# The last tile's embedding rows gathered in two halves of 64 rows per field

## The chip, the core and the metric

The kernel runs on one core of one Trainium2 chip. The metric is the device time of one execution in microseconds (us); lower is better. The core has TensorE (PE, matrix products; its weight loads are shown as PEld), VectorE (DVE), ScalarE (ACT), GpSimd (POOL) and SyncE (SP), and 16 DMA engines that all queues share. Each engine works through its own list of instructions in order, and semaphores order the engines against each other.

## The reference

A recommendation model's top. For each of 512 samples, 26 embedding rows of 128 floats are looked up, one dense row is added, and the products of all pairs of these 27 vectors (351 numbers) and the dense row go through three layers.

```python
e = jnp.stack([tbl_0[ids[:, 0]], ..., tbl_25[ids[:, 25]]], axis=1)     # 512 x 26 x 128
combined = jnp.concatenate([e, r_dense_x[:, None, :]], axis=1)
interact = jnp.einsum('bfd,bgd->bfg', combined, combined)
z = interact[:, _TRIU_I, _TRIU_J]                                      # 512 x 351
h = jnp.concatenate([z, r_dense_x], axis=1)
h = jnp.maximum(h @ W_top1 + b_top1, 0.0)
h = jnp.maximum(h @ W_top2 + b_top2, 0.0)
y = h @ W_top3
```

## The kernel before

The batch is cut into 4 tiles of 128 samples (TILES, P). Ten fields with small tables (LOOK_FIELDS) are looked up on TensorE for all tiles at once: whole tables are brought in, DVE and ACT make one-hot matrices, and PE multiplies (look_up, line 286). That fills the first half of the run. The other 16 fields (GATHER_FIELDS, NG = 16) are gathered by GpSimd: for each tile and field one indirect DMA (line 262) fetches 128 rows of 512 bytes, row p of the tile to partition p of `rows`, by the row numbers in one column of `ids_rows`. These 64 gathers start when `ids_rows` has landed (one transfer at the head of SP's queue, line 225) and follow each other with no other wait, tile 0 first. They are all that GpSimd does after its constants.

Sixteen fields are four groups of four (GROUP = 4, NGROUPS = 4). `rows_landed[t][g]` counts 16 for each gather of a group. `turn(t, g)` on PE waits for 16 * GROUP of it (line 305), turns the four 128x128 blocks (line 307) into PSUM, and ACT's `save_turn(t, g)` copies them into `vecs` (line 597). When all four groups of a tile are saved, `gram` makes the pair products (line 321), DVE's `pack` transposes and picks them (lines 489 and 503), `turn_pairs` (line 344) turns them, and the three layers follow: `layer1_dense` (332), `layer1_pairs` (352), `layer2` (362), `layer3` (371).

The order on PE is written out by hand and interleaves tiles. For the last tile (t = 3) it is: gram(2, 1), layer3(1), turn(3, 0), keep_clock(2), turn_pairs and layer1_pairs of tile 2, turn(3, 1), layer2(2, both), turn(3, 2), layer1_dense(3), layer3(2), turn(3, 3), gram(3, both), keep_clock(4), and then the pairs and layers of tile 3 alone to the end. `keep_clock` (line 377) multiplies zeros so that PE isn't idle while DVE packs. ACT's order is by hand too: save_turn(3, 0) stands ahead of save_pairs(2), save_turn(3, 1) ahead of save_h2(2), save_turn(3, 3) ahead of save_pairs(3). SP's last instruction waits for all four tiles' results (y_saved) and writes them out (line 247).

Of the kernel before, what the change touches and what calls it, by code (L numbers as in the profile page):

```python
# [7 lines left out]
I32 = mybir.dt.int32  # L8
# [3 lines left out]
P = 128  # L12
TILES = 4
# [9 lines left out]
GATHER_FIELDS = [f for f in range(FIELDS) if f not in LOOK_FIELDS]  # L23
NL = len(LOOK_FIELDS)
NG = len(GATHER_FIELDS)
# [32 lines left out]
GROUP = 4  # L58
# [51 lines left out]
def turn_index(t, g):  # L110

    return 1 + t * NGROUPS + g


def build(nc, ids_gather, ids_look, x, tables, looks, w1, b1, w2, b2, w3, out):
    with ExitStack() as ctx:
        def sb(name, shape, dt=F32):
            return ctx.enter_context(nc.sbuf_tensor(name, shape, dt))

        def sem(name):  # L120
            return ctx.enter_context(nc.semaphore(name))
# [2 lines left out]
        zeros = sb("zeros", [P, P])  # L124
        row_ids = sb("row_ids", [P, len(CHUNK_KINDS), MAX_CHUNKS])
        minus_ids = sb("minus_ids", [P, len(CHUNK_KINDS), MAX_CHUNKS])
        ids_rows = sb("ids_rows", [P, TILES * NG], I32)
        ids_wide = sb("ids_wide", [P, WIDE_HELD, 2 * BATCH], I32)

        with nc.sbuf_tensor("table", [P, ARENA, D], F32) as table:  # L130
# [5 lines left out]
        rows = sb("rows", [P, TILES * NG, D])  # L136
# [26 lines left out]
        rows_landed = [[sem(f"rows_landed{t}_{g}") for g in range(NGROUPS)] for t in range(TILES)]  # L163
# [86 lines left out]
        @block.gpsimd  # L250
        def _(pool):
            for n, chunks in enumerate(CHUNK_KINDS):
                nc.gpsimd.iota(row_ids[:, n, 0:chunks], pattern=[[1, chunks]], base=0, channel_multiplier=chunks,
                               allow_small_or_imprecise_dtypes=True).then_inc(consts_ready, 1)
            nc.gpsimd.memset(ident[:], 0.0).then_inc(blank, 1)
            pool.wait_ge(blank, 1)
            nc.gpsimd.affine_select(out=ident[:], in_=ident[:], compare_op=ALU.not_equal, fill=1.0, base=0,
                                    pattern=[[-1, P]], channel_multiplier=1).then_inc(consts_ready, 1)
            pool.wait_ge(ids_landed, 16)
            for t in range(TILES):  # L260
                for i in range(NG):
                    nc.gpsimd.indirect_dma_start(  # L262
                        rows[:, t * NG + i, :], None, tables[GATHER_FIELDS[i]],
                        bass.IndirectOffsetOnAxis(ap=ids_rows[:, t * NG + i:t * NG + i + 1], axis=0)
                    ).then_inc(rows_landed[t][i // GROUP], 16)

        @block.tensor
        def _(pe):
            def look_up(j):

                if j >= 2:
                    pe.wait_ge(look_saved, j - 1)
                head = HEAD_STEPS if j == 0 else 1
                order = [(f, name, k) for name in ("high", "low") for f in range(2) for k in range(head)]
                order += [(f, name, k) for k in range(head, STEPS[j]) for f in range(2) for name in ("high", "low")]
                for f, name, k in order:
                    i = 2 * j + f
                    if f == 0 and name == "high":
                        if k < DVE_STEPS[j]:
                            pe.wait_ge(hot_dve, DVE_STEP0[j] + k + 1)  # L280
                        else:
                            pe.wait_ge(hot_act, ACT_STEP0[j] + k - DVE_STEPS[j] + 1)
                    if k == 0:
                        pe.wait_ge(high_ready if name == "high" else low_ready, i + 1)
                    weights = part(high if name == "high" else low, i)[:, k, :]
                    mm = nc.tensor.matmul(look_ps[:, j % 2 * 2 + f, :], weights,  # L286
                                          onehot[:, (STEP0[j] + k) % RING, f * BATCH:(f + 1) * BATCH],
                                          start=(name == "high" and k == 0),
                                          stop=(name == "low" and k == STEPS[j] - 1))
                    if f == 1 and name == "low":  # L290
                        mm.then_inc(step_used, 1)
                    if j == COUPLES - 1 and f == 1 and name == "low" and k % 2 == 1 and k < 2 * NGROUPS:
                        turn(0, k // 2)
# [7 lines left out]
            def turn(t, g):  # L301
                n = turn_index(t, g)

                pe.wait_ge(turn_saved, n - 1)
                pe.wait_ge(rows_landed[t][g], 16 * GROUP)
                for i in range(GROUP):
                    mm = nc.tensor.transpose(turn_ps[:, n % 2, i * P:(i + 1) * P],  # L307
                                             rows[:, t * NG + g * GROUP + i, :], ident[:])
                mm.then_inc(turned, 1)
# [82 lines left out]
            for j in range(1, COUPLES):  # L392
                look_up(j)

            turn(1, 0)
            pe.wait_ge(look_saved, COUPLES)
            pe.wait_ge(last_look_saved, 1)
            gram(0, 0)
            turn(1, 1)
            pe.wait_ge(w1_landed, 16)  # L400
            layer1_dense(0)
# [326 lines left out]
```

## Time and profile before

| | us |
|---|---|
| median of 3 runs | 114.54 (114.31 to 116.4) |
| the profiled execution | 115.43 |
| its span, first to last instruction | 113.6 |
| PE busy | 100.8 (89% of the span) |
| PEld busy | 84.9 (75%) |
| POOL busy | 68.6 (60%) |
| DVE busy, ACT busy | 53.2, 49.1 |

The profiled execution spent 115.43 - 113.6 = 1.83 us outside the span. Times in the views count from the first instruction. Idle time of an engine that doesn't set the end costs nothing, so the views to read are those that say what the engine on the path waited for, and when each transfer was in place.

### The profile page before, as it was taken

What the parts mean: (1) busy time and instruction counts of PE and PEld (TensorE: products, weight loads), DVE (VectorE), ACT (ScalarE), POOL (GpSimd) and SP (SyncE); (2) the same over time, 40 slices, a digit from 0 to 9 for tenths busy, and PEclk for the clock granted to TensorE, in tenths of its full rate; (3) what the DMA queues carried; (4) which work ended last, traced back from release to release, by engine and by line L of the source; (5) the groups of instructions that cost most, each with busy time, mean ns of one, the idle gap of its engine ahead of it and who ended that gap; (6) DMA issues with size and microseconds to landing.
All of it is one profiled execution on the core that took longest, in us unless ns stands there. A gap on an engine that the chain in (4) does not pass through costs nothing.

```text
span 113.6 us, 3435 instructions
## 1 busy us (share of the span) xinstructions
PE 100.8 (89%) x1538; PEld 84.9 (75%) x1538; DVE 53.2 (47%) x108; ACT 49.1 (43%) x73; POOL 68.6 (60%) x72
## 2 busy tenths in 40 slices
PE   6957999999975999999998969999999989883992
PEld 6943788888854788688778759887989789682890
DVE  1019989999949685980010083116220443007130
ACT  4422553994374759529942151015331313500122
POOL 3277777777778777877777777777677730000000
PEclk9999589999997699999999999999999999999999
DMA  2999955947962899411211221221222210000000
GB/s 77 349 358 398 369 192 163 265 141 239 319 239 48 244 389 344 135 46 46 72 49 52 59 68 46 52 72 49 52 46 74 53 46 0 6 6 0 6 0 1
DMA packets 6001, 14.68 MB, mean 129 GB/s; under 512 B 1889, under 2 KB 2913, under 8 KB 5858
## 3 DMA queue, kind: packets, MB, share of 16 engines
q1 hardware_dynamic: 3650, 9.22, 22.4%
q0 software_dynamic: 2048, 4.20, 14.4%
q10 hardware_dynamic: 288, 1.05, 2.6%
q8 instruction: 12, 0.20, 0.7%
q14 instruction: 3, 0.02, 0.1%
HBM read 14.45 MB, written 0.00 MB: 127 GB/s over the span
## 4 chain that ended last, share of the span: by engine, by line
PE 68%; DMA 10%; ACT 8%; issue 6%; DVE 5%; SPq 0%; DVEq 0%
PE look_ps L286 27%; PE gram_ps L321 12%; PE look_ps L352 10%; PE look_ps L362 7%; DMA ids_wide<-ids_look_dram 6%; PE turn_ps L307 5%; DMA table<-tbl_dram 4%; PE look_ps L332 3%; ACT apart L573 3%; ACT onehot L576 3%; DVE onehot L481 2%; DVE dots L489 2%; PE look_ps L344 1%; PE look_ps L371 1%; PE look_ps L377 1%
## 5 line engine op out<-in xcount | busy, mean ns | idle before, releaser
L262 POOL DMA_INDIRECT rows<-tbl_dram,ids_rows x64 | 67.7, 1058 | 22.6 <-issue 19.2
L286 PE MATMUL look_ps<-onehot,high 128*128 128x512 f32 x88 | 35.6, 421 | 4.4 <-ACT onehot L576 2.4
L286 PE MATMUL look_ps<-onehot,low 128*128 128x512 f32 x88 | 34.5, 415 | 0.0
L481 DVE TENSOR_SCALAR onehot<-ids_wide,row_ids 128x1024 fp32r<-128x1024 int32 x37 | 25.8, 748 | 9.0 <-DMA ids_wide<-ids_look_dram 6.7
L286 PEld LDWEIGHTS look_ps<-onehot,high 128*128 128x128 f32 x88 | 17.1, 197 | 9.7 <-ACT onehot L576 3.2
L286 PEld LDWEIGHTS look_ps<-onehot,low 128*128 128x128 f32 x88 | 18.1, 205 | 3.9
L559 ACT CAST high<-table 128x1024 fp32r<-128x1024 f32 (+1 forms) x10 | 11.2, 1136 | 8.8 <-DMA table<-tbl_dram 8.8
L489 DVE STREAM_TRANSPOSE dots<-gram_ps 128x352 f32<-128x352 f32 (+2 forms) x12 | 5.6, 465 | 19.7 <-PE gram_ps L321 19.7
L471 DVE TENSOR_TENSOR low<-table,high 128x1024 fp32r<-128x1024 f32 (+1 forms) x10 | 13.1, 1319 | 2.5 <-ACT high L559 2.5
L321 PE MATMUL gram_ps<-vecs 128*27 128x27 f32 x1024 | 12.8, 195 | 1.6 <-ACT vecs L597 0.7
L321 PEld LDWEIGHTS gram_ps<-vecs 128*27 128x27 f32 x1024 | 10.9, 108 | 3.8 <-issue 1.1
L597 ACT COPY vecs<-turn_ps 128x512 f32<-128x512 f32 x16 | 9.3, 592 | 9.0 <-PE turn_ps L307 8.9
L352 PE MATMUL look_ps<-pairs_t,w_sb 128*128 128x128 f32 x96 | 12.0, 276 | 0.2 <-ACT pairs_t L603 0.2
L352 PEld LDWEIGHTS look_ps<-pairs_t,w_sb 128*128 128x128 f32 x96 | 11.5, 193 | 0.5 <-ACT pairs_t L603 0.5
L573 ACT ACTIVATE apart<-ids_wide,minus_ids 128x1024 f32<-128x1024 int32 x7 | 8.1, 1152 | 5.3 <-PE look_ps L286 4.0
L307 PE MATMUL turn_ps<-ident,rows 128*128 128x128 f32 x64 | 9.8, 278 | 0.0
L307 PEld LDWEIGHTS turn_ps<-ident,rows 128*128 128x128 f32 x64 | 7.2, 141 | 1.5 <-issue 0.4
L362 PE MATMUL look_ps<-h,w_sb 128*128 128x128 f32 x64 | 8.3, 280 | 0.0
L362 PEld LDWEIGHTS look_ps<-h,w_sb 128*128 128x128 f32 x64 | 7.6, 191 | 0.3 <-DVE h L516 0.2
L576 ACT ACTIVATE onehot<-apart 128x1024 fp32r<-128x1024 f32 x7 | 7.4, 1061 | 0.2
L583 ACT COPY vecs<-look_ps 128x1024 f32<-128x1024 f32 x4 | 4.4, 1091 | 6.8 <-PE look_ps L286 6.8
L608 ACT ACTIVATE h<-look_ps,b_sb 128x128 f32<-128x128 f32 x8 | 2.5, 364 | 9.2 <-PE look_ps L352 9.2
(37 smaller groups left out, 53.5 us busy)
## 6 DMA issues: line engine op xcount, KB each, us to landing
ids_wide<-ids_look_dram SPq DMA_DIRECT2D x5, 512.0 KB, 4.0
table<-tbl_dram SPq DMA_DIRECT2D x4, 640.0 KB, 5.5
table<-tbl_dram SPq DMA_DIRECT2D x4, 512.0 KB, 10.4
table<-tbl_dram ACTq DMA_DIRECT2D x2, 512.0 KB, 5.3
rows<-tbl_dram,ids_rows POOLq DMA_INDIRECT x64, 3.5
w_sb<-w_dram SPq DMA_DIRECT2D x1, 1024.0 KB, 8.5
w_sb<-w_dram SPq DMA_DIRECT2D x1, 512.0 KB, 7.6
x_rows<-x_dram SPq DMA_DIRECT2D x1, 256.0 KB, 10.0
```

Source lines behind the costliest of these rows:

```text
L262: nc.gpsimd.indirect_dma_start(rows[:, t * NG + i, :], None, tables[GATHER_FIELDS[i]], bass.IndirectOffsetOnAxis(ap=ids_rows[:, t * NG + i ...
L286: mm = nc.tensor.matmul(look_ps[:, j % 2 * 2 + f, :], weights, onehot[:, (STEP0[j] + k) % RING, f * BATCH:(f + 1) * BATCH], start=(name == ...
L307: mm = nc.tensor.transpose(turn_ps[:, n % 2, i * P:(i + 1) * P], rows[:, t * NG + g * GROUP + i, :], ident[:])
L321: mm = nc.tensor.matmul(gram_ps[32 * j:32 * j + SLOTS, b, q * SLOTS:(q + 1) * SLOTS], v, v, start=True, stop=True)
L352: mm = nc.tensor.matmul(h1_cols(n), w1_sb[:, c, n * P:(n + 1) * P], pairs_t[:, c, :], start=False, stop=(c == PAIR_CHUNKS - 1), skip_group ...
L362: mm = nc.tensor.matmul(look_ps[:, m, 0:P], w2_sb[:, n, m * P:(m + 1) * P], h1[:, n, :], start=(n == 0), stop=(n == N1 - 1))
L471: nc.vector.tensor_tensor(part(low, i), part(table, i), part(high, i).bitcast(F32), ALU.subtract).then_inc(low_ready, 1)
L481: nc.vector.tensor_scalar(onehot[:, q % RING, :], ids_wide[:, j % WIDE_HELD, :], row_ids[:, kind(j), k:k + 1], None, ALU.is_equal).then_in ...
L559: copy(part(high, i), part(table, i)).then_inc(high_ready, 1)
L573: nc.scalar.activation(apart[:], ids_wide[:, j % WIDE_HELD, :], ACT.Abs, bias=minus_ids[:, kind(j), k:k + 1]).then_inc(apart_ready, 1)
L576: nc.scalar.activation(onehot[:, q % RING, :], apart[:], ACT.Relu, bias=1.0, scale=-1.0).then_inc(hot_act, 1)
L597: copy(tile_vecs(t, slice(s, s + GROUP)), turn_ps[:, n % 2, :].rearrange("p (s b o) -> p b s o", s=GROUP, o=2)).then_inc(turn_saved, 1)
```

## The change

For tile 3 each field is gathered by two indirect DMAs of 64 rows instead of one of 128: first the rows of partitions 0 to 63 for all 16 fields, then those of partitions 64 to 127 for all 16. The row numbers are read from partitions 0 to 63 in both cases, so `ids_rows` has 16 more columns (80 instead of 64), in which the second half's numbers stand at partitions 0 to 63; the host lays them out. `turn(3, g)` waits for twice the count. Tiles 0 to 2 are gathered as before, and the orders on PE, DVE, ACT and SP are the same.

```diff
-        ids_rows = sb("ids_rows", [P, TILES * NG], I32)
+        ids_rows = sb("ids_rows", [P, (TILES + 1) * NG], I32)
...
-            for t in range(TILES):
+            for t in range(TILES - 1):
                 for i in range(NG):
                     nc.gpsimd.indirect_dma_start(
                         rows[:, t * NG + i, :], None, tables[GATHER_FIELDS[i]],
                         bass.IndirectOffsetOnAxis(ap=ids_rows[:, t * NG + i:t * NG + i + 1], axis=0)
+                    ).then_inc(rows_landed[t][i // GROUP], 16)
+
+            t = TILES - 1
+            for half in range(2):
+                for i in range(NG):
+                    at = (t + half) * NG + i
+                    nc.gpsimd.indirect_dma_start(
+                        rows[half * P // 2:(half + 1) * P // 2, t * NG + i, :], None, tables[GATHER_FIELDS[i]],
+                        bass.IndirectOffsetOnAxis(ap=ids_rows[0:P // 2, at:at + 1], axis=0)
                     ).then_inc(rows_landed[t][i // GROUP], 16)
...
-                pe.wait_ge(rows_landed[t][g], 16 * GROUP)
+                pe.wait_ge(rows_landed[t][g], 16 * GROUP * (2 if t == TILES - 1 else 1))
...
+    gather_ids = ids[:, GATHER_FIELDS].reshape(TILES, P, NG)
+    gather_ids = np.concatenate([gather_ids, np.roll(gather_ids[-1:], P // 2, axis=1)])
...
-        "ids_gather": ids[:, GATHER_FIELDS].reshape(TILES, P, NG).transpose(1, 0, 2).reshape(P, -1),
+        "ids_gather": gather_ids.transpose(1, 0, 2).reshape(P, -1),
```

## Rows read from the trace of the kernel before

**Rows 1.** The page: the chain that ended last, by engine.

```profile
PE 68%; DMA 10%; ACT 8%; issue 6%; DVE 5%; SPq 0%; DVEq 0%
```

**Rows 2.** Waits, 86 to 100 us: who waited for whom, us, times, longest.

```profile
ACT vecs L597 <- PE turn_ps L307: 0.7, 2, 0.3
...
PEld turn_ps L307 <- issue: 0.4, 2, 0.2
```

**Rows 3.** The page: the gathers' group (busy, mean ns, idle before) and their queue.

```profile
q0 software_dynamic: 2048, 4.20, 14.4%
...
L262 POOL DMA_INDIRECT rows<-tbl_dram,ids_rows x64 | 67.7, 1058 | 22.6 <-issue 19.2
```

**Rows 4.** Line 262 from 72 to 94 us: ns min/median/max; landing from issue.

```profile
L262 POOL DMA_INDIRECT rows<-tbl_dram,ids_rows x17: 940/944/947, 71.1 to 91.1; - x17
...
DMA to landing us min/median/max: 2.5/2.6/3.5
```

**Rows 5.** Timeline of POOL: first and last of the last tile's 16 gathers.

```profile
72.32 0.94 POOL L262 DMA_INDIRECT rows<-tbl_dram,ids_rows  x1 [0.30 <-issue]
...
91.06 0.94 POOL L262 DMA_INDIRECT rows<-tbl_dram,ids_rows  x1 [0.30 <-issue]
```

**Rows 6.** Timeline, 82 to 114 us, PE's and ACT's instructions around the turns of tile 3.

```profile
88.95 0.60 PE L371 MATMUL look_ps<-h,w_sb 128*1 128x128 f32 x4
...
89.47 0.66 PE L307 MATMUL turn_ps<-ident,rows 128*128 128x128 f32 x4
...
90.78 0.27 ACT L603 COPY pairs_t<-look_ps 128x128 f32<-128x128 f32 x1
...
91.41 1.06 PE L352 MATMUL look_ps<-pairs_t,w_sb 128*128 128x128 f32 x8
...
94.20 0.60 PE L307 MATMUL turn_ps<-ident,rows 128*128 128x128 f32 x4
...
96.42 0.60 PE L307 MATMUL turn_ps<-ident,rows 128*128 128x128 f32 x4
...
98.38 0.66 PE L307 MATMUL turn_ps<-ident,rows 128*128 128x128 f32 x4
...
99.07 0.59 ACT L597 COPY vecs<-turn_ps 128x512 f32<-128x512 f32 x1 [0.33 <-PE turn_ps L307]
99.71 2.35 PE L321 MATMUL gram_ps<-vecs 128*27 128x27 f32 x256 [0.68 <-ACT vecs L597]
```

**Rows 7.** DMA queues from 72 to 94 us: all packets, and the gathers' own.

```profile
DMA packets 550, 1.18 MB, mean 54 GB/s; under 512 B 274, under 2 KB 274, under 8 KB 546
...
q0 software_dynamic: 546, 1.12, 20.4%
```

**Rows 8.** Timeline: GpSimd's shortest instruction, and SP's transfer of the row numbers.

```profile
0.27 0.10 POOL L717 MEMSET const-float32-1.0<- 128x1 f32 x1
...
0.74 0.40 SPq L225 DMA_DIRECT2D ids_rows<-ids_gather_dram  x1
```

**Rows 9.** Windows: stretch, length, busy of PE PEld DVE ACT POOL, PEclk, DMA, GB/s.

```profile
7.27:10.00 2.73, 1.00 (x2) 0.37 (x2) 1.97 (x3) 1.05 (x1) 2.12 (x3) 1.00 1.02 416
...
11.24:14.52 3.28, 3.28 (x10) 2.55 (x9) 3.13 (x4) 1.81 (x2) 2.67 (x3) 0.54 1.07 371
33.37:35.49 2.12, 0.00 (x2) 0.00 (x1) 2.12 (x3) 2.03 (x2) 2.10 (x1) 0.98 0.17 43
35.49:38.83 3.34, 3.34 (x8) 2.66 (x9) 2.74 (x4) 1.23 (x2) 2.42 (x4) 0.50 0.75 205
98.30:113.60 15.30, 10.50 (x317) 8.82 (x315) 3.54 (x14) 2.52 (x8) 0.00 (x0) 1.00 0.01 2
```

**Rows 10.** Timeline near the end: DVE's packing, the idle stretch inside keep_clock, tile 3's pairs.

```profile
103.56 0.30 DVE L503 COPY pairs<-dots 128x64 f32<-128x64 f32 x2
...
104.34 0.94 PE L377 MATMUL look_ps<-zeros 128*128 128x128 f32 x6 [1.86 <-issue]
105.11 0.38 PE L344 MATMUL look_ps<-ident,pairs 128*128 128x128 f32 x2
```

## The prediction

> **What bounds the kernel now.** I read the chain that ended last first: it is PE for 68% of the span [rows 1]. So the question is whether PE ever waits for gathered rows. The waits between 86 and 100 us, where the last tile's rows are turned, answer it: before the turns PEld waited 0.4 us for "issue" and never for a DMA, and it is ACT that waits for the turns [rows 2]. So the rows of tile 3 are in place when PE wants them. How early they are is the cover that this change spends, and it comes from three views.
>
> The gathers alone: in the last stretch each takes 944 ns on GpSimd [rows 4], and 0.30 us passes before the next [rows 5]. The 16 of tile 3 start from 72.32 to 91.06, 1.25 us apart: 15 x 1.25 = 18.7. (Earlier gathers are slower, 1058 ns on the mean of all 64 [rows 3]; tiles 0 to 2 are not touched.) A gather lands 2.6 us after its start at the median, 2.5 at the least [rows 4], so 1.6 us after GpSimd is through with it; I use that 1.6 for the small ones too. The last rows are therefore there at 91.06 + 0.94 + 1.6 = 93.6.
>
> PE's own needs: the turns of groups 0 to 3 start at 89.47, 94.20, 96.42 and 98.38 [rows 6]. The last group has 98.38 - 93.6 = 4.8 us in hand. After turn(3, 3) nothing of another tile is left: ACT's save, gram and the layers follow in a line, 113.6 - 98.4 = 15.2 us, at a granted clock of 1.00 [rows 6, 9]. Each us by which the last turn is late is a us at the end.
>
> **The change part by part.** Removed: 16 gathers of 128 rows. Added: 32 of 64 rows. With T the time of a small one and the same 0.30 us after each (the gap is the same 0.30 throughout [rows 5]), the last starts at 72.32 + 31 x (T + 0.30) and lands T + 1.6 later, at 83.22 + 32 x T. It delays the turn at 98.38 by 32 x (T - 0.474). Everything hangs on T, for which no row exists: all gathers of this trace have 128 rows.
>
> Bounds. Above: a smaller gather should not take longer than a large one, T = 0.944. Below: all of it goes by rows, T = 0.47, and then the delay is nothing, since 32 halves cost as much as 16 wholes did plus 16 x 0.30 = 4.8 us of gaps, just the 4.8 us in hand. Two nearer bounds come from what a gather is made of. GpSimd's shortest instruction takes 0.10 us [rows 8], so some of the 0.944 can't go by rows. And of the 546 packets of the gathers in this stretch half are under 512 bytes, though a row has 512 [rows 7]; 2048 packets for 64 gathers are 32 each [rows 3]: one with rows and one small one for each of 16 engines. A half gather still pays both on 16 engines. If the time goes by entries, 64 + 16 against 128 + 16, T is 0.944 x 80 / 144 = 0.525; if by packets, 32 against 32, it is 0.944. I have no row to choose between these and take the middle, T = 0.735: a period of 1.035 us.
>
> By that, group g (complete after 20 + 4g gathers, because all the first halves stand ahead of all the second) is there at 72.32 + (19 + 4g) x 1.035 + 0.735 + 1.6, that is at 94.3, 98.5, 102.6 and 106.7. What is queued behind turn(3, 0): on PE keep_clock and all of tile 2's pairs and layers, on ACT save_pairs(2) behind save_turn(3, 0). PE is free for it from about 89.3, so it idles some 5.0 us and then starts at 94.3. In the way before, turn 0 to turn 1 took 94.20 - 89.47 = 4.7 us, of which up to 0.3 is slack (ACT's copy ends at 91.05 and line 352 starts at 91.41), and the next two steps 2.2 and 2.0 [rows 6]. So turn 1 comes near 98.9, turn 2 at 102.6 (the rows; PE alone would be there at 101.1) and turn 3 at 106.7 (PE alone 104.6). The last gather rules: delay 106.7 - 98.4 = 8.4 us.
>
> **TensorE's clock.** PE now has idle stretches: about 5.0 us before turn 0, about 1.5 and 2.1 before turns 2 and 3, and 0.68 before gram. In this trace, 1.00 us busy of 2.73 from 7.27 to 10.00, and nothing busy for 2.12 us from 33.37, were each followed by a stretch of 3.3 us at the lower level, 1.2 GHz (0.54 and 0.50) [rows 9]. One such stretch costs up to half its length, 1.7 us. The one after the wait for turn 0 is hidden: turns 1 and 2 would be about as late as their rows (turn 1 at 98.9 + 1.7 = 100.6, turn 2 at 102.8), and turn 3 still waits. The one that could follow the wait for turn 3 lies in gram and the layers, uncovered. But 1.86 us idle at 102.5, with 0.68 shortly before, passed with no drop [rows 9, 10]. I take half a chance of 1.7 us: 0.8.
>
> **Small parts.** The transfer of row numbers grows by 16 columns, 8 KB of 40; the first gather starts with it, but no turn of tiles 0 to 2 waits on rows, and its place in SP's queue is the same single issue of 0.40 us [rows 8]: nothing. PE's doubled count is the same instruction. The 1.86 us "issue" gap in keep_clock [rows 10] lies partly under DVE's packing; if the long wait gives PE's instructions time to arrive, up to 1.2 us of it comes back (the pairs are packed at 103.86 and PE turns them at 105.11 [rows 10]). I leave it in the sum and in the range.
>
> **Sum.** 8.4 + 0.8 = 9.2 us. Against the profiled execution: 113.6 + 9.2 + 1.83 = 124.6. That execution is 0.9 above the median of the runs, 114.54, so the forecast is 114.54 + 9.2 = 123.7.
>
> The Trainium skill speaks against this change (DMA: Bandwidth & Descriptors, Rules for kernel authors): two transfers to disjoint halves of the partitions aren't worth it, since both run over the same 16 engines, and one of 128 partitions should be used. It names the DMA engines as the reason; here they are busy only 20.4% of the stretch [rows 7], and by that reason alone the sum would be nothing.
>
> **Rivals.**
> - The price goes by rows (T near 0.47 to 0.525). For it: each row needs its own read and write entry, and the fixed gap of 0.30 is already outside T. Against it: the 16 engines' small packets and the 0.10 of an empty instruction. With T = 0.47 the last rows land at 98.3, just when PE turns them, and group 0 at 72.32 + 19 x 0.77 + 0.47 + 1.6 = 89.0, ahead of 89.47: no change, 114.5. With T = 0.525 the delay is 1.6, 116.2. It is slower by 2% (2.3 us) from T = 0.545 on. This is the case that ends on the other side.
> - The price is fixed (T near 0.944). For it: the count of packets doesn't fall with the rows, and all gathers of the quiet stretch take 940 to 947 ns whatever table they read [rows 4]. Against it: 128 entries must cost something. Delay 32 x 0.47 = 15.0; PE idles 9 us before turn 0 and about 3 before turns 2 and 3, so a low stretch in the end becomes likely: 129.6, and 131.3 with 1.7 of clock. The Trainium skill leans this way (DMA: Bandwidth & Descriptors, Anatomy of one DMA): descriptor generation is called small, and many descriptors can be emitted before the extra cost shows. By it the time is this rival's; no run yet shows it.
> - The clock decides: both halves of the tail at the lower level, two stretches of 3.3 us, 3.3 us more than the 8.4: 126.3. It needs idle stretches as long as the two of [rows 9]; that is in the range.
> - The change is without effect because PE doesn't notice: that is the first rival, since the cover is 4.8 us. A gain has no place to come from but the 1.2 us of the issue gap, with T at its lower bound: 113.3.
>
> **How the numbers follow.** T between 0.6 and 0.87 (delays of 4.0 and 12.7, so 118.6 to 127.2 with the clock left aside): 0.60, of which 0.07 for the rival of the clock; forecast 123.7. T above: 0.25. T from 0.545 to 0.6: 0.06. T below 0.545, the first rival, within 2%: 0.08. Faster by over 2%: 0.01. A difference of 2% is about what a measurement of this kernel tells from none. Slower: 0.91. Range: from 117.5, T of 0.57, to 131.0, full price with most of a clock stretch; it leaves out the first rival and little else.
>
> **What would show it.** In the profile after: line 262 x32 on its new line with a mean that is T; PE (or PEld) at line 307 waiting for "DMA rows" before turns 0, 2 and 3, in all near 8.4 us; the last gather's start near 72.32 + 31 x (T + 0.30); about 15.2 us from the last turn to the end; a granted clock below 1.00 after 94. Wrong would make it: a gap other than 0.30 between small gathers, a landing far from 1.6 us after GpSimd's part, or T near an end of its bounds.

## The result, and the profile after

| | before | after |
|---|---|---|
| median, us | 115.47 (114.31 to 119.03, 4 runs) | 130.55 (130.18 to 130.69, 4 runs) |
| ratio to before | | 1.1365, 95% interval 1.1288 to 1.1442 |
| profiled execution | 115.43 | 130.18 |
| its span | 113.6 | 128.4 |

The ratio leaves out executions in a slower state that some runs of any kernel fall into, so it isn't the quotient of the medians. The change costs 14.8 us of span in the profiled executions, and 1.78 us lie outside it, where 1.83 did before. The lines of the page that answer to [rows 1, 3], with the engines' totals and the granted clock in 40 slices (the line of 262 is now tiles 0 to 2, line 271 the halves, 316 the turns, 330 gram, 361 layer1_pairs, 386 keep_clock):

```profile
PE 105.1 (82%) x1538; PEld 88.4 (69%) x1538; DVE 53.1 (41%) x108; ACT 49.2 (38%) x73; POOL 80.8 (63%) x88
...
PEclk9999999999999977999999999999975799859599
...
q0 software_dynamic: 2560, 4.20, 11.9%
...
POOL 61%; issue 21%; PE 10%; DMA 5%; ACT 1%; POOLq 1%
...
L262 POOL DMA_INDIRECT rows<-tbl_dram,ids_rows x48 | 51.1, 1066 | 17.3 <-issue 14.3
...
L271 POOL DMA_INDIRECT rows<-tbl_dram,ids_rows x32 | 28.8, 900 | 9.8 <-issue 9.8
```

The chain that ended last has changed engines: it was PE for 68% [rows 1], and is now GpSimd for 61%, with most of its 21% of issue being the 0.30 us gaps between gathers. The kernel is bound by the string of gathers from the first one on. The price that the prediction lacked is in the last line: a gather of 64 rows takes 900 ns, against 944 for 128 [rows 4].

The view of line 271 alone, and the first and last of its instructions in GpSimd's timeline, to be held against [rows 4, 5]:

```profile
L271 POOL DMA_INDIRECT rows<-tbl_dram,ids_rows x32: 893/901/907, 70.5 to 107.8; - x32
...
who waited for it (us, times):
  PE turn_ps L316: 9.0, 3
...
DMA to landing us min/median/max: 2.2/2.4/4.0
...
70.47 0.90 POOL L271 DMA_INDIRECT rows<-tbl_dram,ids_rows  x1 [0.30 <-issue]
...
107.83 0.90 POOL L271 DMA_INDIRECT rows<-tbl_dram,ids_rows  x1 [0.30 <-issue]
```

31 steps from 70.47 to 107.83 are 1.205 us each. The last rows land 2.3 us after that, at 110.1, and nothing but PE waits for them. PE's timeline from the first turn of tile 3 on, to be held against [rows 6, 10]:

```profile
95.87 1.09 PE L316 MATMUL turn_ps<-ident,rows 128*128 128x128 f32 x4 [5.82 <-DMA rows<-tbl_dram,ids_rows]
...
102.63 0.60 PE L316 MATMUL turn_ps<-ident,rows 128*128 128x128 f32 x4
...
105.59 0.63 PE L316 MATMUL turn_ps<-ident,rows 128*128 128x128 f32 x4 [0.57 <-DMA rows<-tbl_dram,ids_rows]
...
110.25 0.63 PE L316 MATMUL turn_ps<-ident,rows 128*128 128x128 f32 x4 [2.62 <-DMA rows<-tbl_dram,ids_rows]
...
111.56 1.79 PE L330 MATMUL gram_ps<-vecs 128*27 128x27 f32 x130 [0.68 <-ACT vecs L606]
...
113.70 1.61 PE L330 MATMUL gram_ps<-vecs 128*27 128x27 f32 x126 [0.36 <-issue]
115.24 0.49 PE L386 MATMUL look_ps<-zeros 128*128 128x128 f32 x2
...
118.61 0.64 PE L353 MATMUL look_ps<-ident,pairs 128*128 128x128 f32 x2
```

The last turn moved from 98.38 to 110.25: 11.87 us. From the last turn to the end it was 15.22 us (113.6 - 98.38) and is 18.15 (128.4 - 110.25): 2.93 more. The two make the 14.8. By pieces, the 2.93 are: gram's start to the first keep_clock 2.29 before (99.71 to 102.00) and 3.68 now, +1.39; from there to turning the pairs 3.11 and 3.37, +0.26; from the pairs to the end 8.49 and 9.79, +1.30; the turn itself the same. The granted clock stands beside two of these (windows: stretch, length, busy of PE, PEld, DVE, ACT, POOL, PEclk, DMA share, GB/s):

```profile
111.56:113.35 1.79, 1.79 (x130) 1.66 (x130) 0.00 (x0) 0.00 (x0) 0.00 (x0) 0.50 0.00 0
119.00:121.00 2.00, 1.86 (x9) 1.61 (x8) 0.00 (x0) 0.48 (x2) 0.00 (x0) 0.50 0.03 8
```

### The profile page after: what moved, and what is told of

The parts are those of the page before. It is cut to its first block, busy times and chain, and to the rows that moved or that the text cites. A ratio compares the mean times of both kernels' runs of the same rounds, so it can differ in the third digit from the quotient of the medians.

```text
span 128.4 us, 3451 instructions
## 1 busy us (share of the span) xinstructions
PE 105.1 (82%) x1538; PEld 88.4 (69%) x1538; DVE 53.1 (41%) x108; ACT 49.2 (38%) x73; POOL 80.8 (63%) x88
## 3 DMA queue, kind: packets, MB, share of 16 engines
q0 software_dynamic: 2560, 4.20, 11.9%
## 4 chain that ended last, share of the span: by engine, by line
POOL 61%; issue 21%; PE 10%; DMA 5%; ACT 1%; POOLq 1%
POOL rows L262 40%; POOL rows L271 21%; PE look_ps L361 3%; DMA ids_rows<-ids_gather_dram 3%; PE gram_ps L330 3%; DMA rows<-tbl_dram,ids_rows 2%; PE look_ps L371 2%; PE look_ps L386 1%; POOLq L116 1%; PE turn_ps L316 0%; ACT vecs L606 0%; PE look_ps L353 0%; PE look_ps L380 0%; ACT h L622 0%; ACT pairs_t L612 0%
## 5 line engine op out<-in xcount | busy, mean ns | idle before, releaser
L262 POOL DMA_INDIRECT rows<-tbl_dram,ids_rows x48 | 51.1, 1066 | 17.3 <-issue 14.3
L295 PE MATMUL look_ps<-onehot,high 128*128 128x512 f32 x88 | 34.9, 411 | 5.6 <-ACT onehot L585 4.0
L271 POOL DMA_INDIRECT rows<-tbl_dram,ids_rows x32 | 28.8, 900 | 9.8 <-issue 9.8
L295 PE MATMUL look_ps<-onehot,low 128*128 128x512 f32 x88 | 33.7, 403 | 0.0
L295 PEld LDWEIGHTS look_ps<-onehot,low 128*128 128x128 f32 x88 | 17.0, 194 | 3.8 <-DVE low L480 0.3
L316 PE MATMUL turn_ps<-ident,rows 128*128 128x128 f32 x64 | 10.4, 291 | 9.0 <-DMA rows<-tbl_dram,ids_rows 9.0
L330 PE MATMUL gram_ps<-vecs 128*27 128x27 f32 x1024 | 13.7, 202 | 2.5 <-issue 0.9
L330 PEld LDWEIGHTS gram_ps<-vecs 128*27 128x27 f32 x1024 | 11.6, 116 | 4.7 <-issue 2.0
L361 PE MATMUL look_ps<-pairs_t,w_sb 128*128 128x128 f32 x96 | 14.5, 310 | 0.3
L361 PEld LDWEIGHTS look_ps<-pairs_t,w_sb 128*128 128x128 f32 x96 | 13.7, 225 | 1.1 <-ACT pairs_t L612 1.1
L520 DVE COPY pairs_t<-look_ps 128x128 f32<-128x128 f32 x4 | 1.2, 291 | 14.7 <-PE look_ps L353 14.7
```

What stands on the lines that cost most here:

```text
L262: nc.gpsimd.indirect_dma_start(rows[:, t * NG + i, :], None, tables[GATHER_FIELDS[i]], bass.IndirectOffsetOnAxis(ap=ids_rows[:, t * NG + i ...
L271: nc.gpsimd.indirect_dma_start(rows[half * P // 2:(half + 1) * P // 2, t * NG + i, :], None, tables[GATHER_FIELDS[i]], bass.IndirectOffset ...
L330: mm = nc.tensor.matmul(gram_ps[32 * j:32 * j + SLOTS, b, q * SLOTS:(q + 1) * SLOTS], v, v, start=True, stop=True)
L361: mm = nc.tensor.matmul(h1_cols(n), w1_sb[:, c, n * P:(n + 1) * P], pairs_t[:, c, :], start=False, stop=(c == PAIR_CHUNKS - 1), skip_group ...
```

## The experiments

Two questions were put to the experiments. What does a gather cost, by its rows, by its engines, or by being an instruction? And what makes the stretch behind the last turn 2.9 us longer? Several runs of the changed kernel stood beside the experiments:

> The changed kernel once more, beside the others of this set. Expected: ratio to before near 1.137 as in its first runs, line 271 x32 with a mean near 900 ns, span near 128.4 us, and again about 18 us from the last turn (line 316) to the end, with two stretches of granted clock near 0.50 in it.

Measured: 131.7 us (129.49 to 132.08), with no ratio; span 129.8, line 271 at 893/900/914 ns, last turn at 111.66, so 18.1 us from it to the end.

> The changed kernel beside the next two: ratio to before 1.13 to 1.145, time near 130.5.

Measured: 130.05 us (128.59 to 131.39), ratio 1.137 (1.115 to 1.159); last turn at 111.01 of 127.8, 16.8 us to the end.

> The changed kernel beside them: last turn to the end 16.8 to 18.2 us, gram and its first gap together 3.4 to 3.8 us (with a clock near 0.50 in it), last gather's end to last turn 1.5 us.

Measured, one run: 130.26 us, last turn at 110.68 of 128.4, 17.7 to the end, gram with its gap 3.73 us. So the stretch behind the last turn varies from 16.8 to 18.2 us over four traces of one kernel, and differences below 1.4 us in it say little by themselves.

**What a gather costs by its rows.** The kernel before, with twelve gathers behind its own:

```diff
+PROBE_SIZES = [128, 96, 64, 48, 32, 16, 8, 4, 120, 100, 68, 64]
...
+            for m, n in enumerate(PROBE_SIZES):
+                nc.gpsimd.indirect_dma_start(
+                    probe[0:n, m, :], None, tables[GATHER_FIELDS[0]],
+                    bass.IndirectOffsetOnAxis(ap=ids_rows[0:n, 0:1], axis=0)).then_inc(probed, 16)
```

> The kernel before, with 12 more gathers behind its 64 that nobody but the last instruction of SP waits for, of 128, 96, 64, 48, 32, 16, 8, 4, 120, 100, 68 and 64 rows in this order. It prices a gather by its rows, apart from everything else. Theory A (a price for the instruction, 0.7 ns for a row): from 944 ns at 128 and 900 at 64 the line is 857 + 0.69 x rows, so 923, 900, 890, 879, 868, 862, 860 ns for 96, 64, 48, 32, 16, 8, 4 rows. Theory B (the price is for the share of each DMA engine, and falls when fewer engines have one): the same down to 16 rows, then about half at 8 rows (430 ns) and a quarter at 4, and less at 100 and 68 rows than at 96 and 64. Theory C (my prediction's middle, half by entries): 735 ns at 64 rows and 630 at 32; the changed kernel's trace already speaks against it. The time should be that of before or up to 2 us more, as the last probe ends near 108.

Measured: 117.2 us, one run. The view of the probe's line, asked for each instruction's own stretch (ns min/median/max, start in us), in the order 128, 96, 64, 32, 16, 8, 4, 100, 68, 64 rows (48 rows took 877 ns and 120 took 999):

```profile
L272 POOL DMA_INDIRECT probe<-tbl_dram,ids_rows x1: 944/944/944, 92.7 to 92.7; - x1
L272 POOL DMA_INDIRECT probe<-tbl_dram,ids_rows x1: 939/939/939, 93.9 to 93.9; - x1
L272 POOL DMA_INDIRECT probe<-tbl_dram,ids_rows x1: 921/921/921, 95.2 to 95.2; - x1
...
L272 POOL DMA_INDIRECT probe<-tbl_dram,ids_rows x1: 875/875/875, 97.6 to 97.6; - x1
L272 POOL DMA_INDIRECT probe<-tbl_dram,ids_rows x1: 854/854/854, 98.8 to 98.8; - x1
L272 POOL DMA_INDIRECT probe<-tbl_dram,ids_rows x1: 882/882/882, 99.9 to 99.9; - x1
L272 POOL DMA_INDIRECT probe<-tbl_dram,ids_rows x1: 887/887/887, 101.1 to 101.1; - x1
...
L272 POOL DMA_INDIRECT probe<-tbl_dram,ids_rows x1: 1021/1021/1021, 103.6 to 103.6; - x1
L272 POOL DMA_INDIRECT probe<-tbl_dram,ids_rows x1: 1109/1109/1109, 104.9 to 104.9; - x1
L272 POOL DMA_INDIRECT probe<-tbl_dram,ids_rows x1: 918/918/918, 106.4 to 106.4; - x1
```

From 128 rows down to 16 the price falls by 90 ns, 0.8 ns a row, and at 8 and 4 rows it is 30 ns up again. Theory A holds within 30 ns for the nine gathers whose rows are 128, 96, 64, 48, 32, 16, 8 and 4, but not for 120, 100 and 68 rows, which took 59, 95 and 205 ns more than its line. B is wrong at both of its ends (8 and 4 rows are not cheap, 100 and 68 are the dearest); C is out. Each size was measured once (64 rows twice). The 64 rows took 920 here and 900 in the changed kernel, and neither that nor the three dear sizes is explained by this probe.

**Twice the rows, as many instructions.** In the last tile each field is gathered whole, twice:

```diff
-            for half in range(2):
+            for again in range(2):
...
-                        rows[half * P // 2:(half + 1) * P // 2, t * NG + i, :], None, tables[GATHER_FIELDS[i]],
-                        bass.IndirectOffsetOnAxis(ap=ids_rows[0:P // 2, at:at + 1], axis=0)
+                        (spare if again == 0 else rows[:, t * NG:, :])[:, i, :], None, tables[GATHER_FIELDS[i]],
+                        bass.IndirectOffsetOnAxis(ap=ids_rows[:, t * NG + i:t * NG + i + 1], axis=0)
```

> The last tile's rows by 32 gathers of 128 rows, the first 16 into a spare tile that nobody reads, the second 16 as in before; the wait is for both. It moves twice the rows of the changed kernel with as many instructions. Theory (a price for the instruction, hardly one for the rows): 32 x 0.043 = 1.4 us more than the changed kernel, a span of 129.5 to 131. Rival (moving the rows costs as well, through the DMA engines): clearly more, 134 or above.

Measured, one run: 130.96 us, span 129.1. The last gather starts at 110.12 and the last turn at 112.84, 2.6 us later than in the changed kernel's first profile. The forecast of 1.4 was too small by about 1 us, because the last tile's gathers started at 71.42 here and at 70.47 there (more on these starts below); the rival's 134 is not seen. Twice the bytes cost the 44 ns by which each instruction is longer (944 against 900) and little else. From the last turn to the end it is 16.3 us here.

**Half the rows, half the instructions.** Only the first halves; the rows of partitions 64 to 127 are left out. Zeros stand there; the line with which DVE writes them is not shown here.

```diff
-            for half in range(2):
+            for half in range(1):
...
-                pe.wait_ge(rows_landed[t][g], 16 * GROUP * (2 if t == TILES - 1 else 1))
+                pe.wait_ge(rows_landed[t][g], 16 * GROUP)
```

> The changed kernel with only the first halves of the last tile gathered: 16 gathers of 64 rows instead of 32; the rows of partitions 64 to 127 are left out (DVE writes zeros there once, in a stretch in which it waits). The row numbers keep the wide layout and the gathers keep their 64 rows. Theory (what costs is the number of gathers, at 1.205 us each with the gap): the last one starts 0.6 us earlier than in the kernel before, PE waits for no rows, and the time is that of before within 1%. Rival (something else about gathers of 64 rows, such as a later landing or work of other engines beside them, costs): half of the loss or more stays, 6 us or more above before.

Measured: 118.07 us (115.58 to 119.36) beside 117.7 (113.83 to 118.25) of before, run next to it, too scattered for a ratio. The best runs of each, 115.58 against 113.83, are 1.8 us apart: "within 1%" isn't shown, but the rival's 6 us are out. The trace decides more sharply on the gathers: the 16 start from 70.93 to 89.01 and nobody waits for them. Gathers of 64 rows delay nothing as such; their number does. One thing in this trace matters for the second question: its last turn is at 99.14, PE waits for no rows, and yet it is 18.4 us to the end, with a granted clock of 0.53 over 6.5 us of the layers.

**The layout alone.** The kernel before with the 80 columns:

```diff
-        ids_rows = sb("ids_rows", [P, TILES * NG], I32)
+        ids_rows = sb("ids_rows", [P, (TILES + 1) * NG], I32)
```

> The kernel before with only the layout part of the change: ids_rows has 80 columns instead of 64 and is brought so, the gathers are the 64 whole ones. Theory: nothing, within 1% of before; the first gather starts less than 0.1 us later. Rival (the larger transfer delays the chain of gathers, which sets the end of the changed kernel): the first gather starts 0.5 us later or more.

Measured: 115.9 us (115.45 to 116.24) beside the same 117.7 (113.83 to 118.25); the first gather starts at 5.03 us (5.11 in the trace of before), and from the last turn to the end it is 15.3 us. The rival is out: the gathers aren't late. That the layout costs nothing at all can't be read from these times, since the best of before is 1.6 us below the best here; the next experiment, which has the same 80 columns and a ratio of 1.005, gives the closer bound.

**How much the cover holds.** Only the fields in HALVED have two gathers:

```diff
-            for half in range(2):
-                for i in range(NG):
+            for i in range(NG):
+                for half in range(2 if i in HALVED else 1):
...
+                    n = P // 2 if i in HALVED else P
```

The slices of the gather take n rows, and the count that `turn` waits for follows HALVED (both not shown).

> Only the last group's 4 fields of the last tile are halved, each field's halves one after the other: 20 gathers for the tile instead of 16. Theory (4.8 us of cover, each halved field costs 2 x 1.205 - 1.249 = 1.16 us): 4.6 us later than in before, the last rows land at about 98.2 against a turn at 98.4: PE waits under 0.5 us and the time is within 1% of before. Rival (any halving costs, cover or not): 4/16 of the whole loss, about 3.9 us.

Measured, HALVED = 12 to 15: 115.02 us (113.44 to 118.64, 10 runs) beside 114.57; ratio 1.005 (0.998 to 1.012). The last gather starts at 94.91, its rows land at about 97.2, the last turn is at 97.49, and PE's array never idles for rows. Four more gathers delay no turn, though they end within 0.3 us of the cover's end, and the time leaves room for 1.4 us at most. The stretch behind the last turn isn't that of before, though: 17.6 us in the profiled execution (116.97 us, the second slowest of the ten). Its gram, and a window on the layers:

```profile
98.83 1.30 PE L332 MATMUL gram_ps<-vecs 128*27 128x27 f32 x130 [0.68 <-ACT vecs L608]
100.78 1.26 PE L332 MATMUL gram_ps<-vecs 128*27 128x27 f32 x126 [0.65 <-issue]
...
105.50:109.00 3.50, 3.37 (x16) 3.37 (x17) 0.29 (x1) 0.25 (x2) 0.00 (x0) 0.55 0.02 5
```

So a gap in gram and a low clock on the layers can stand there although PE didn't idle for rows.

> The last two groups' 8 fields halved: 24 gathers for the tile. Theory (cover used up at four fields): the last turn is late by (8 - 4) x 1.16 = 4.6 us, and the time 4.5 us above before, or up to 2 us more if the clock falls in the end: ratio 1.035 to 1.06. Rival (proportional): half of the loss, 7.9 us, ratio 1.07.

Measured, HALVED = 8 to 15: 121.44 us (120.64 to 122.27), ratio 1.064 (1.050 to 1.079). The view of the gathers' line:

```profile
L273 POOL DMA_INDIRECT rows<-tbl_dram,ids_rows x24: 893/903/947, 71.8 to 99.9; - x24
...
who waited for it (us, times):
  PE turn_ps L318: 4.1, 1
```

The last turn is at 102.33, 3.95 us later than in before; 4.6 was forecast. The total lies just above the theory's 1.06, with an interval that reaches into its range: from the last turn to the end it is 18.2 us here too. The ratio can't part the theory from the proportional rival (1.07), but the two doses together can: 4 fields cost nothing that the ratio shows, 8 about 7 us, 16 about 15. Past the cover each halved field moves the last turn by 1.2 us, and up to 3 us come on top in the stretch behind it.

**The order of the halves.** A field's two halves one after the other, so that groups 0 to 2 are complete earlier:

```diff
-            for half in range(2):
-                for i in range(NG):
+            for i in range(NG):
+                for half in range(2):
```

> The changed kernel with the two halves of a field one after the other, so that groups 0, 1, 2 are complete after 8, 16, 24 gathers instead of 20, 24, 28; the last after 32 as before. Theory (only the last gather sets the end): with 1.205 us for each the rows of groups 0 and 1 are there at 81.2 and 90.8, in time, those of group 2 at 100.5 and of group 3 at 110.1; PE waits for rows 3 to 4 us and 7 to 8 us, and the end stays within 1 us of the changed kernel, about 130.5 us (ratio to before 1.13 to 1.145). Rival (the order of the halves costs, since it makes turn(3, 0) wait 5.8 us and all behind it): those 5.8 us go, 124.5 us, ratio near 1.08.

Measured: 129.59 us (128.0 to 132.44), ratio 1.118 (1.087 to 1.150), too wide to tell it from the changed kernel; the rival's 1.08 lies just outside. PE's waits in its trace:

```profile
PE turn_ps L316 <- DMA rows<-tbl_dram,ids_rows: 9.1, 2, 7.5
```

The 5.8 us ahead of turn(3, 0) are gone and have come back ahead of turn(3, 3), where PE now idles 7.5. The last gather starts at 108.7 as ever. The earlier waits were no loss of their own.

**The clock behind the last turn.** PE is kept busy with zeros while it waits for the last rows, and for a short while behind the turn:

```diff
             layer3(2)
+            keep_clock(11)
             turn(3, 3)
+            keep_clock(2)
```

> The changed kernel with keep_clock(11) on PE ahead of turn(3, 3), where it idles 2.6 us for the rows, and keep_clock(2) behind that turn; nothing else. Theory (of the 14.8 us, 11.9 are the late turn and 2.9 the lower clock in what follows): with PE busy ahead of the last turn the stretch at 1.2 GHz over gram goes, and perhaps the second one, so the time from the last turn to the end falls from 18.1 to between 16.7 and 15.2 us: 1.4 to 2.9 us less than the changed kernel, 127.6 to 129.1. Rival (the tail is longer for another reason, such as instructions that arrive late after the wait): no change, 130.5, or 0.2 more.

Measured: 130.48 us (129.06 to 130.68), ratio 1.133 (1.116 to 1.150); last turn at 112.16 of 128.9, 16.7 us to the end. PE's timeline of gram, and its window:

```profile
113.47 2.15 PE L330 MATMUL gram_ps<-vecs 128*27 128x27 f32 x232 [0.23 <-ACT vecs L608]
117.73 0.47 PE L330 MATMUL gram_ps<-vecs 128*27 128x27 f32 x24 [2.10 <-issue]
...
113.47:115.62 2.15, 2.15 (x232) 2.05 (x232) 0.00 (x0) 0.00 (x0) 0.00 (x0) 1.00 0.03 8
```

gram's first 232 matmuls take 2.15 us, the pace of before (256 in 2.35 [rows 6]), and the stretch behind the last turn is 1.4 us shorter than in the changed kernel's first profile (and as long as in its third). The total shows none of it, as the last tile's gathers started at 72.44 in this trace, 2.0 us later than there. But the issue gap of 2 us that stood in keep_clock, under DVE's packing, now stands in gram with nothing beside it. The program of PE had been shifted by 13 units of keep_clock, which are 26 matmuls in the profile, and the gap has moved by as many: it stood behind 256 + 2 matmuls from gram's start, and stands behind 232. So the next kernel keeps the place in the program, by leaving out the 11 dummy calls of CODE_SHIFT at PE's start, 22 matmuls in the profile, as many as keep_clock(11) adds:

```diff
-CODE_SHIFT = 11
+CODE_SHIFT = 0
...
             layer3(2)
+            keep_clock(11)
             turn(3, 3)
```

> The changed kernel with keep_clock(11) ahead of turn(3, 3) and, to keep every instruction of PE behind that at its place in the program, the 11 matmuls of CODE_SHIFT at PE's start left out. It repeats the last attempt, in which 2.1 us of idle time called issue had moved from keep_clock into the middle of gram. Theory (lower clock): the issue gap is back inside keep_clock as in before, gram runs at 1.00, and the last turn to the end takes 15.2 us, or 16.9 if the second stretch at 1.2 GHz stays; against 18.1 in the changed kernel the total is 1.3 to 2.9 us less, with the last turn at the same distance behind the last gather. Rival (the lower clock isn't what makes the tail longer): 18 us again.

Measured: 131.46 us (131.21 to 132.53), no ratio; span 129.7, last turn at 111.30, 18.4 us to the end. The theory missed. Its gram in PE's timeline, and the windows:

```profile
112.60 1.30 PE L330 MATMUL gram_ps<-vecs 128*27 128x27 f32 x130 [0.68 <-ACT vecs L607]
115.07 1.27 PE L330 MATMUL gram_ps<-vecs 128*27 128x27 f32 x126 [1.17 <-issue]
...
112.60:113.90 1.30, 1.30 (x130) 1.19 (x130) 0.00 (x0) 0.00 (x0) 0.00 (x0) 1.00 0.00 0
115.07:116.27 1.20, 1.20 (x126) 1.16 (x126) 0.00 (x0) 0.00 (x0) 0.00 (x0) 1.00 0.07 14
```

The clock is 1.00 throughout, and yet gram takes 3.67 us to the first keep_clock, as in the changed kernel (3.68): what the clock gives back is lost in a gap of 1.17 us behind the 130th matmul, where the changed kernel has 0.36 and before has none. At that time the only DMA traffic is the queue called instruction. The page counts 12 loads of it, 0.20 MB in all, for PE's 1538 matmuls, one for every 128. Its bursts of 66 GB/s for 0.25 us, 16 KB each, in the windows, of before:

```profile
98.00:98.25 0.25, 0.25 (x4) 0.12 (x2) 0.00 (x0) 0.00 (x0) 0.00 (x0) 1.00 0.22 66
101.50:101.75 0.25, 0.25 (x53) 0.25 (x43) 0.00 (x0) 0.00 (x0) 0.00 (x0) 1.00 0.29 66
```

and of the changed kernel and the one with the 11 units:

```profile
111.25:111.50 0.25, 0.00 (x0) 0.00 (x0) 0.00 (x0) 0.25 (x1) 0.00 (x0) 1.00 0.23 66
112.25:112.50 0.25, 0.00 (x0) 0.00 (x0) 0.00 (x0) 0.25 (x1) 0.00 (x0) 1.00 0.30 66
```

In before, the first burst comes at 98.0, 1.7 us ahead of gram, and the gap that ends at 104.34 follows the second, at 101.5, by 2.8. In the kernel with the 11 units it comes at 112.25, 0.35 ahead of gram, and PE goes on at 115.07, again 2.8 later. The same holds in the changed kernel: burst at 111.25, PE goes on at 113.70 (2.45); burst at 114.75, PE goes on at 117.71 (2.96). And the first burst comes about 1 us after the last rows have landed in these kernels: 110.1 and 111.25 in the changed one, 111.1 and 112.25 here, 102.2 and 103.5 with eight fields halved, 97.2 and 98.25 with four, where the rows came just in time. Where the rows were early it stands 0.3 to 0.4 us ahead of the last turn (before, one half, the layout alone). I read it as a load of PE's instructions that isn't asked for while PE's queue stands at the wait for rows; nothing here shows the request itself. Two more kernels moved the program by one and two units against this one:

```diff
-            keep_clock(11)
+            keep_clock(12)
```

> As the last busy-wait kernel, but keep_clock(12) ahead of turn(3, 3): every instruction of PE behind it stands one keep_clock unit (two matmuls with their weight loads) later in the program. The traces so far say that a 16 KB load of PE's instructions lands 1.1 us after PE gets past the wait for the last rows, and that what it brings starts with the 131st matmul of gram, where PE idled 1.17 us. Theory (the load is asked for just behind the wait for rows, so it comes late when that wait is long): the gap in gram moves with the program to behind 128 matmuls; if one unit is enough to ask ahead of the wait, the gap goes and gram takes 2.3 to 2.5 us, and the last turn to the end falls from 18.4 to 17.0 or less. Rival (the gap in gram has to do with the turn or the save): it stays behind 130 matmuls, and gram stays at 3.7 us.

Measured, one run: 131.51 us. The gap is behind 128 matmuls, 1.31 us long; the burst at 112.25 again; last turn to the end 18.5.

```diff
-            keep_clock(11)
+            keep_clock(13)
```

> The same with keep_clock(13): two units later. Theory (late load): the request stands ahead of the wait, the first 16 KB are there in time, gram has no gap behind its 126th matmul; the next load's gap falls two matmuls ahead of gram's end instead of two behind it, so gram's last two are about 2 us late, and the tail is shorter by the first gap, 1.2 us, and longer by the part of the second that DVE's packing no longer covers. Rival (not the load): a gap of 1.1 to 1.2 us behind 126 to 130 matmuls of gram as before.

Measured, one run: 132.97 us, 19.2 from the last turn to the end. The gaps of gram in PE's timeline:

```profile
113.33 1.27 PE L330 MATMUL gram_ps<-vecs 128*27 128x27 f32 x126 [0.68 <-ACT vecs L607]
115.58 1.28 PE L330 MATMUL gram_ps<-vecs 128*27 128x27 f32 x128 [0.98 <-issue]
119.30 0.29 PE L330 MATMUL gram_ps<-vecs 128*27 128x27 f32 x2 [2.45 <-issue]
```

The gaps move with the program, matmul by matmul (130, 128, 126), and stand 128 matmuls apart, so they belong to places in the code, not to the turn or the save. That one or two units would bring the request ahead of the wait was wrong. The 13 units of the first attempt seem to have done it: its first gap should stand behind 104 matmuls of gram, and there is none, and no burst between the last turn and 115.25. Where exactly it is asked for stays open.

**What all traces say of the clock.** In the seven traces in which PE idled 2.6 us or more right ahead of the last turn (four of the changed kernel, twice the rows, by field, eight halved), the granted clock was 0.50 in part or all of gram. In the nine others, with the rows in time or PE kept busy, it was 1.00 in gram, but for the 24 and the 2 matmuls that came behind a gap of over 2 us (lines above). So this low stretch goes with the wait, and keeping PE busy took it away. The second one, on the layers, does not follow the wait: it is there with four fields halved and with one half, where PE waited for no rows, and in the kernels kept busy; it is absent in the changed kernel's third trace and with twice the rows, where PE waited. Its cause is not shown. The third trace also shows how the clock and the load go together:

```profile
112.78 3.50 PE L330 MATMUL gram_ps<-vecs 128*27 128x27 f32 x256 [0.68 <-ACT vecs L606]
...
112.00:112.25 0.25, 0.10 (x1) 0.00 (x0) 0.00 (x0) 0.12 (x1) 0.00 (x0) 0.50 0.27 66
112.78:116.21 3.43, 3.42 (x256) 3.23 (x257) 0.00 (x0) 0.00 (x0) 0.00 (x0) 0.50 0.02 5
```

The burst is as late as elsewhere, but at 0.50 the first 130 matmuls take so long that PE reaches the new instructions only when they are there: no gap, 3.43 us. At 1.00 with the gap it is 3.67. The two losses in gram hide each other and don't add. One trace fits neither: behind the probe of sizes gram took 3.50 us at 1.00 with the rows in time, in small pieces of idle time, with GpSimd's extra gathers running beside it. What slowed it is not separated.

## Why the prediction was wrong

The direction and the way were right, and the range held the time, but the loss was put at 9.2 us and is 14.8 of span. The step that failed is the main term of the sum, T, the time of a gather of 64 rows: I had bounds of 0.525 and 0.944 and took the middle, 0.735; it is 0.900. By its own formula, 32 x (0.900 - 0.474), the delay is 13.6 instead of 8.4. That adds 5.3 us; the earlier start and landing (below) take 2.1 off, and the stretch behind the last turn adds 2.1 more than the 0.8 that stood in the sum; the 0.3 that are left to 14.8 are rounding and the 0.15 from the landing to the turn. The count of packets, named as the upper bound's reason, gave the number that was near the truth, and it can be read off the queue: 2560 packets for 80 gathers are 32 each, as for whole ones [rows 3]. But packets are not shown to be the cause; the probe shows only that rows are hardly charged. The middle between the two bounds had nothing behind it, and the reason for the upper bound, that a smaller gather shouldn't take longer than a large one, held at 64 rows but not at 120, 100 and 68.

- **Cover of 4.8 us:** right, and shown by dose: four fields halved, 4.6 us, delayed no turn and gave a ratio of 1.005.
- **Start of the last tile's gathers:** taken as 72.32, it was 70.47. That takes 1.85 off: 1.4 because the 48 gathers ahead took 1066 ns on the mean instead of 1095, and 0.4 because the first one started at 4.69 instead of 5.11. In the traces here the start lies between 70.5 and 72.7; in before such a shift is hidden, in the changed kernel it goes into the time.
- **Gap of 0.30 us, landing 1.6 us after GpSimd's part:** the gap is right, the landing of the last rows is 1.4. With T and the start, the rows are there at 70.47 + 31 x 1.205 + 0.90 + 1.39 = 110.1, and the turn follows at 110.25.
- **Waits ahead of turns 0, 2, 3:** 5.8, 0.6 and 2.6, as told in kind (5.0, 1.5, 2.1). That the last gather rules and the earlier waits don't add was right, and shown by the order of the halves.
- **Clock:** priced at half a chance of 1.7 us. Measured, the stretch behind the last turn took 2.9 us more in the first profile and 1.6 to 2.9 over four. The mechanism was part of it: a low stretch lay on gram after every such wait, and a second one on the layers in three of the four, whose tie to the wait is not shown. What I had missed is that a load of PE's instructions also comes late in these kernels, which costs as much in gram when the clock is full.
- **The issue gap in keep_clock:** expected to shrink by up to 1.2 us under a long wait. It is 1.98 in the first profile and 1.33 to 1.57 in the three others, against 1.86, and behind a gram that is over 1 us longer. A long wait gave nothing back here: by the reading above it holds the load back.
- **Columns added, doubled count:** nothing, as said, as far as the ratio of 1.005 of the kernel with four fields halved can tell.

The rival of the fixed price came closest: 129.6 without clock, 131.3 with it, 130.55 measured. It had a chance of 0.25. Its total is close partly by luck: its delay of 15.0 us was 3.1 too long, and the stretch behind the last turn, which it left at 15.2 or priced with 1.7 of clock, made up for it. The Trainium skill says (DMA: Bandwidth & Descriptors, Anatomy of one DMA) that descriptor generation is small and that many descriptors can be emitted before the extra cost shows. The probe agrees for the rows, with 90 ns between 16 and 128, though the instruction itself is far from small here, 0.85 us and 0.30 of gap. The Trainium skill's rule against two transfers to disjoint partition halves (DMA: Bandwidth & Descriptors, Rules for kernel authors) is borne out in the outcome, but not for the reason that it gives, the shared DMA engines: twice the bytes through them changed little, and the issuing engine was the bound.

## What to carry to other kernels

Price indirect gathers by their count: here 1.2 us of GpSimd each, whether it fetched 16 rows or 128 (and up to 1.4 at three odd counts), so split one only within the cover that the trace shows, and compute that cover (landing of the last one against its use) before anything else. Once a queue has become the chain that ends last, every early delay in it counts to the end. A wait on PE can cost more than its length: look behind it for a lower granted clock and for a late instruction load, and take both away before judging either, since each can hide the other. And look at several traces of each kernel before you tie what stands behind a wait to the wait.

## What the runs showed of the hardware

- A gather of 8 or 4 rows (882, 887 ns) is no cheaper than one of 16 (854), and those of 120, 100 and 68 rows cost 999, 1021 and 1109 ns, more than 128 rows at 944. Each was measured once.
- Loads on the queue called instruction, 16 KB each, are visible as bursts of 66 GB/s in quiet windows; PE went on 2.4 to 3.0 us after the burst that I take it to have needed, and gaps of the name issue stood 128 matmul and weight-load pairs apart in the code.
- With the clock at 1.00 gram took as long as at 0.50 (3.67 us with an issue gap of 1.17, against 3.68 with one of 0.36 and 3.43 with none). In the one kernel with a late turn in which both the low clock and the gap were away from its first 232 matmuls, they ran at the pace of before.
- The granted clock was 0.50 in part or all of gram in all seven traces with an idle PE ahead of the last turn, and 1.00 there in the nine others, but for what came behind a gap of over 2 us.
